# The wait in the edge scatters of a graph network: the last group of eight instead of the group four back

## The reference

```python
edge_index = jnp.stack([src, dst])
x = x + _L0_gnn_ref(_layernorm(x), src, dst, edge_weight, ...)     # relu(segment_sum(val * x[src]) @ W)
x = x + _L0_ffn_ref(_layernorm(x)[None], ...)[0]                   # 16 experts, top 2
x = x + _L1_gnn_ref(_layernorm(x), src, dst, edge_weight, ...)
x = x + _L1_ffn_ref(_layernorm(x)[None], ...)[0]
x = x + _L2_gnn_ref(_layernorm(x), src, dst, ...)                  # attention, softmax per destination
x = x + _L2_ffn_ref(_layernorm(x)[None], ...)[0]
x = x + _L3_gnn_ref(_layernorm(x), edge_index, edge_weight, ...)   # three rounds of sums over neighbours
x = x + _L3_ffn_ref(_layernorm(x)[None], ...)[0]
```

## Time and profile before

| | us |
|---|---|
| median of 3 runs | 6919.58 |
| fastest and slowest of them | 6911.33, 6929.57 |
| the profiled execution, its own time | 6900.21 |
| its span, first to last instruction | 6898.5 |
| GpSimd busy in it | 2226.9 |
| TensorE busy in it | 5202.9 |

### The profile page before, as it was taken

One profiled execution on the slowest core, in us unless ns is written; L12 is line 12 of the kernel. 1 busy time (PEld: TensorE's weight loads), 2 busy tenths in 40 slices (PEclk: granted clock), 3 DMA queues, 4 the chain that ended last, 5 costly groups with the idle time before them and its releaser, 6 DMA issues. The chain is left out here.

```text
span 6898.5 us, 86638 instructions
## 1 busy us (share of the span) xinstructions
PE 5202.9 (75%) x22758; PEld 3404.8 (49%) x22807; DVE 2801.3 (41%) x6714; ACT 1456.7 (21%) x3735; POOL 2226.9 (32%) x2209
## 2 busy tenths in 40 slices
PE   3521649898785979568888668888688599999944
PEld 2410337645772459445554445554587544444443
DVE  4271459801323042447666456666323301010142
ACT  1220215401120013113333213333232210000020
POOL 3357120054354515146664055564003200000024
PEclk9999999998797979779998779998788799999957
DMA  0000003253463416468887178887115632424233
GB/s 15 1 1 1 1 26 133 122 176 130 145 200 126 133 53 214 129 201 291 279 285 232 40 240 272 273 275 219 55 44 160 194 126 83 168 80 168 80 87 113
DMA packets 484682, 960.54 MB, mean 139 GB/s; under 512 B 112649, under 2 KB 292468, under 8 KB 481718
## 3 DMA queue, kind: packets, MB, share of 16 engines
q1 hardware_dynamic: 324902, 640.54, 27.7%
q0 software_dynamic: 114208, 281.05, 13.5%
q10 hardware_dynamic: 45296, 35.56, 1.7%
HBM read 737.19 MB, written 219.74 MB: 139 GB/s over the span
## 5 line engine op out<-in xcount | busy, mean ns | idle before, releaser
L1213 PE MATMUL banks<-ring,xn 128*128 128x512 f32 (+1 forms) x3500 | 1348.8, 548 | 121.0 <-PEq L133 104.5
L1040 POOL DMA_INDIRECT rows<-pairs,idxr x832 | 937.1, 1126 | 603.6 <-DVE prod L1991 363.0
L1213 PEld LDWEIGHTS banks<-ring,xn 128*128 128x128 f32 x3500 | 627.9, 191 | 842.7 <-issue 825.7
L2105 PE MATMUL banks<-agg,hotT 128*128 x1664 | 498.6, 435 | 185.2 <-DVE prod L1991 101.2
L394 POOL DMA_INDIRECT dst_table<-nodes_pay,nodes_row x392 | 386.6, 986 | 775.6 <-DVEq L1187 407.2
L394 POOL DMA_INDIRECT bin_table<-bins_pay,bins_row x392 | 403.5, 1029 | 593.1 <-ACTq L802 204.7
L2105 PEld LDWEIGHTS banks<-agg,hotT 128*128 128x128 f32 x1664 | 328.1, 213 | 270.6 <-issue 219.6
L2208 ACT ACTIVATE x<-banks x832 | 325.1, 391 | 477.6 <-PE banks L2121 349.8
L1687 PE MATMUL banks<-second,hT 128*128 x1544 | 390.7, 393 | 41.5 <-DVE bins_pay L1733 15.8
L1672 PE MATMUL banks<-xT,w1r 128*128 128x128 f32 x3088 | 404.2, 284 | 17.1 <-DVE xT L1725 7.9
L1672 PEld LDWEIGHTS banks<-xT,w1r 128*128 128x128 f32 x3088 | 382.9, 200 | 21.1 <-issue 13.5
(11 more groups left out here) (379 smaller groups left out, 7614.7 us busy)
## 6 DMA issues: line engine op xcount, KB each, us to landing
ring<-adjacency SPq DMA_DIRECT2D x145, 1280.0 KB
spill<-rows SPq DMA_DIRECT2D x208, 512.0 KB
vals<-spill SPq DMA_DIRECT2D x208, 512.0 KB
w1r<-in_L_ffn_W SPq DMA_DIRECT2D x114, 512.0 KB
adjacency<-strips SPq DMA_DIRECT2D x13, 3200.0 KB
w1r<-in_L_ffn_w SPq DMA_DIRECT2D x65, 512.0 KB
rows<-home_rows SPq DMA_DIRECT2D x35, 640.0 KB
ring<-adjacency SPq DMA_DIRECT2D x25, 640.0 KB
```

The costliest lines, as they stand in the source:

```text
L1040: nc.gpsimd.indirect_dma_start(rows[:, row, :], None, table, bass.IndirectOffsetOnAxis(ap=idxr[:, at + g:at + g + 1], axis=0))\
L1213: last = nc.tensor.matmul(K.ps[2 * (g % 2) + o][:, 0:wd], x[:, t * D + o * P:t * D + (o + 1) * P], ring.buffer[:, n % R, 0:wd // cols, q * ...
L2105: last = nc.tensor.matmul(queries(c, part)[:, n % 2 * D:(n % 2 + 1) * D], hotT[:, c % 2, n * P:(n + 1) * P], tile_of(q, at[n]), start=True ...
```

## The change

Two lines of `Scatter.columns` change. Before the first column of each group but the very first, GpSimd now waits on the semaphore of the group just sent, for all that was ever sent on it. Since each earlier group was waited for in the same way, at that point every scatter of the table has landed.

```diff
             h = c // 8 % 4
-            if c % 8 == 0 and self.sent[h]:
-                pool.wait_ge(self.landed[h], 16 * self.sent[h])
+            if c % 8 == 0 and c:
+                pool.wait_ge(self.landed[(h - 1) % 4], 16 * self.sent[(h - 1) % 4])
             self.sent[h] += 1
```

## The result

| | before | after |
|---|---|---|
| median of the runs, us | 6916.42 (4 runs) | 6843.48 (4 runs) |
| fastest and slowest, us | 6911.33, 6929.57 | 6817.74, 6855.57 |
| span of the profiled execution, us | 6898.5 | 6831.3 |

The ratio is 0.9887, with a 95% interval of 0.9852 to 0.9922: the change makes the kernel 1.1% **faster**, where I had given 6923.5 us and faster a chance of 0.03.

What follows compares the result with a forecast made beforehand. It took the cost to lie only where GpSimd ends a stage: 1.9 us in `number_pieces` plus 2.0 us in `load_nodes`, +3.9 us on a 6919.6 us median, 6923.5 us, range 6907 to 6941 us.

Steps and rivals of the forecast that it cites:

- faster: Rival: fewer scatters in flight free DMA engines or VectorE; no mechanism given over 10 us; chance 0.03.
- other engines see GpSimd only at that barrier: At the new waits: behind them come only further scatters and the stage's closing barrier; an idle-engine wait costs 0.95 us.
- The first row: Window of the first part of the nodes' ranking: GpSimd needs 48 of 81 us, so four waits fit.
- The 205 us of the earlier trace: End of the nodes' ranking: GpSimd idles 205 us after c = 349, far longer than its waits could fill.
- leave GpSimd idle at their end for far longer than their waits could fill: Ranking of bins (c = 0 to 119) and last part of nodes' (c = 194 to 349): waits add nothing.
- The forecast of no change: Whole kernel: a change within 0.3%, 20.8 us, counts as the same; chance 0.91.
- The price of a wait: At each new wait with idle DMA engines: 0.95 us net, between bounds of 0.69 and 1.9 us.
- `number_pieces`: Stage of c = 350 to 361, ended by GpSimd: waits at c = 352 and 360 add 1.9 us.
- `load_nodes`: Stage of c = 368 to 378, ended by GpSimd: the wait at c = 376, beside the load of x, adds 2.0 us.
- The fixed 2.0 us of the Trainium skill: Alternative rule for the three waits on the path: fixed cost per GpSimd DMA whatever runs beside it, 2.9 us instead of 3.9.
- The products did not fall behind: Rival in the two matrix products: landings take twice 3.8 us, exceeding 4.2 us of slack, 122 us, 7042 us; chance 0.02.
- GpSimd held by VectorE: Rival in the second part of the nodes' ranking: restarted scatters held 13.1 us each, up to 53 us, 6973 us; chance 0.04.

Runs made afterwards that it cites:

- again: The changed kernel run again, against the kernel before on a chip where that takes 6900.29 us: 6830.34 us, ratio 0.9903.
- again3: The changed kernel once more, against the kernel before on a chip where that takes 6459.84 us: 6526.21 us, ratio 1.009.
- apart: Kernel before with no scatter beside the ranking's two position parts, 276 moved beside the first layer norm: 6952.76 us, ratio 1.0093 to the kernel before.
- units3: Kernel before, with every third scatter of the position parts waiting for the ranking's progress: ratio 0.9705 where the kernel before took 6894.06 us, 1.0027 where 6459.77 us.
- doses: Kernel before, GpSimd in the nodes' position part also waiting for its last scatter at every 2nd, 4th, 12th, then never: 6800.64 us, ratio 0.9845.

## Why the prediction was wrong

- **The step that failed** is the sentence "other engines see GpSimd only at that barrier". From it followed that a wait beside a stage can only cost, that the stages' lengths are given, and that "faster" needed the DMA engines or VectorE. The engine that was freed is TensorE, which the prediction never considered. It had 70 us to win in the ranking, where the text asked only whether the waits fit.
- **A sign was on the page.** The first row has no engine near its 81 us: TensorE 21.6, VectorE 47.8, ScalarE 37.1, GpSimd 48 with its gaps. I used the difference as slack for GpSimd and didn't ask who then ends the stage. The 205 us of the earlier trace rows are the ranking catching up after the scatters have stopped; I read them as cover.
- **That the position parts "leave GpSimd idle at their end for far longer than their waits could fill"** is true on this chip, and only because of the crawl. On chips without it GpSimd ends those parts and most of the 48 waits are on the path, +0.9 to +1.0%. The forecast of no change is thus wrong on both kinds of chip, with opposite signs.
- **The price of a wait**, 0.95 us, was 1.10 us: the completion takes about 0.4 us behind the last packet, if packets and start are as in the earlier trace rows, not 0.25. (The busy slices there are 12 to 14, not 12 to 15, so the last packet may be through at 0.70 us; the completion is then nearer 0.5 us.) `number_pieces` 1.9 forecast, +2.1 measured; `load_nodes` 2.0 forecast, +2.3 measured. Both terms of the sum were there and a little small.
- **The fixed 2.0 us of the Trainium skill** (DMA: Bandwidth & Descriptors, Anatomy of one DMA — SWDGE (gpsimd) path), counted from the issue, fits the idle case: 0.97 + 1.40 - 0.24 = 2.1 us. In `load_nodes` the same difference is 0.96 + 3.04 - 0.24 = 3.8 us, so there it does not hold. The traces side with adding the load.
- **The products did not fall behind.** The 44 waits of the second table, most of them in the products, took 122.7 us, 2.8 us each and 5.4 at most: above the 3.8 us that I took for one at times, under it on average, and neither product is longer than before.
- **GpSimd held by VectorE** was put in the wrong stage, and it happened once: in combine's layer norm the scatter after the third wait took 6.42 us, and GpSimd ended the stage some 5 us late (46.1 us against 41 before and 40 in again). The prediction had "33 of 41" there and hidden waits.

```profile
2052.47 6.42 POOL L394 DMA_INDIRECT dst_table<-nodes_pay,nodes_row  x1 [1.41 <-DMA dst_table<-nodes_pay,nodes_row]
```

  In the second trace of the changed kernel no scatter there took over 1.6 us, so this is chance and no part of the gain or the loss as a rule.

What stays open: why unbroken indirect scatters of GpSimd slow each instruction of TensorE to 1.40 us on some chips and not on others; and what lies behind the ranking. Of the 305 us between the traces of again and again3, the changed kernel on either kind of chip, 240 lie before the last scatter of `bin_table`, 36 in attention's two stretches of gathers (L1040) and 28 in the last expert layer, where GpSimd gathers and scatters rows (L1643, L1649). These too are indirect transfers in long runs beside TensorE, but that they are the crawl again isn't shown.

## What to carry to other kernels

If no engine is busy for the length of a stage, ask first who ends it; background work that seems free may be what stretches it, and leaving it out once (as apart does) shows that in one run. Pace background work of GpSimd by the progress of what it runs beside: units3 gives -3.0% where the change gives -1.0 to -1.1%, and costs 0.3% where the change costs 0.9%. Then look at what the pace does: meant as threes, the scatters went in sixes and nines. Fours with a wait for their landing left the units nearly untouched (doses); in both position parts at once, on a chip that crawls, they weren't tried. And a result of one chip can turn its sign on another: note the time of the unchanged kernel there before reading a ratio.

## What the runs showed that I had not expected

- Beside an unbroken run of indirect scatters, an instruction of TensorE, weight load or matmul, takes 1.40 us until others see it done, and a unit of 58 of them takes 80 us instead of 4.06 us, on three of the five chips that can be told apart in these runs.
- The recorded start of a matmul says little there: in the crawl others were released by it 67 and 77 us after that start.
- Two to four scatters in a row with a pause of 1.4 us leave it nearly untouched (4.1 to 4.8 us a unit), twelve raise it to 5.6 to 17.1 us.
- 78 plain transfers of the same number of packets, issued by GpSimd at 0.53 us, cost TensorE nothing; the indirect ones take 0.97 us each to issue.
